# Four graph layers on one core: TensorE's loaded offsets without their comparisons against bounds

## The reference

```python
x = _layernorm(x + _L0_gnn_ref(x, src, dst, ...), axis=-1)      # degree-normed sum, then an MLP with gelu
x = _layernorm(x + _L1_gnn_ref(x, ..., src, dst, edge_type_8), axis=-1)   # relational attention, one head
x = _layernorm(x + _L2_gnn_ref(x, src, dst, ...), axis=-1)      # (1 + eps) * x + sum, then an MLP with relu
x = _layernorm(x + _L3_gnn_ref(x, edge_attr_64, src, dst, ...), axis=-1)  # attention, four heads, edge scores
```

## Time and profile before

| | us |
|---|---|
| median of 3 runs | 12608.17 (12603.52 to 12621.22) |
| the profiled execution, its own time | 12556.69 |
| its span on the core | 12555.0 |
| PE busy with matmuls | 4294.8 (34%) |
| ACT busy | 3446.0 (27%) |
| POOL busy | 6450.9 (51%) |
| DVE busy | 1628.9 (13%) |

### The profile page before, as it was taken

One profiled execution on the slowest core, in us unless ns is written; L12 is line 12 of the kernel. 1 busy time (PEld: TensorE's weight loads), 2 busy tenths in 40 slices (PEclk: granted clock), 3 DMA queues, 4 the chain that ended last, 5 costly groups with the idle time before them and its releaser, 6 DMA issues. The chain is left out here.

```text
span 12555.0 us, 93986 instructions
## 1 busy us (share of the span) xinstructions
PE 4294.8 (34%) x19065; PEld 3850.4 (31%) x19066; DVE 1628.9 (13%) x3883; ACT 3446.0 (27%) x9383; POOL 6450.9 (51%) x6784
## 2 busy tenths in 40 slices
PE   6233333352222232232244444444512222222222
PEld 5233332341222222222244444444412222222222
DVE  6000000013010110110100000000221111121113
ACT  1333333342222222222223223233312222222222
POOL 1666666656445445445355555555454444444442
PEclk6555555555555555555555555555555555555555
DMA  3111111112000000000111111111210111000110
GB/s 90 23 22 22 22 23 22 22 40 63 18 17 19 17 17 19 17 17 19 27 38 41 41 40 38 41 42 41 53 38 20 20 21 20 20 20 19 21 20 18
DMA packets 333875, 360.12 MB, mean 29 GB/s; under 512 B 172933, under 2 KB 205783, under 8 KB 330425
## 3 DMA queue, kind: packets, MB, share of 16 engines
q0 software_dynamic: 217552, 231.94, 9.4%
q1 hardware_dynamic: 116254, 127.34, 3.2%
HBM read 314.78 MB, written 46.51 MB: 29 GB/s over the span
## 5 line engine op out<-in xcount | busy, mean ns | idle before, releaser
L1037 POOL DMA_INDIRECT rows_a<-table,idx_c_a x3320 | 3166.1, 954 | 3380.4 <-ACT neg_c_a L999 2388.2
L839 POOL DMA_INDIRECT rows_l<-table,idx_c_l x3320 | 3140.1, 946 | 2349.8 <-ACT neg_c_l L793 1264.0
L587 PE MATMUL acc_l<-rows_l,hot_l 128*128 128x65 f32 x6640 | 1638.4, 419 | 2075.8 <-ACT hot_l L743 1226.6
L587 PEld LDWEIGHTS acc_l<-rows_l,hot_l 128*128 128x128 f32 x6640 | 1510.0, 328 | 2215.4 <-issue 2182.3
L587 PE MATMUL acc_a<-msg_a,hot_a 128*128 128x66 f32 (+1 forms) x6640 | 1612.1, 426 | 699.9 <-issue 520.7
L741 ACT ACTIVATE dist_a<-iota,neg_c_a 128x128 bf16<-128x128 f32 x3320 | 1050.9, 387 | 2664.3 <-remote 2286.5
L587 PEld LDWEIGHTS acc_a<-msg_a,hot_a 128*128 128x128 f32 x6640 | 1476.6, 328 | 833.0 <-issue 829.5
L1221 PE MATMUL work_a<-ident,tail_a 48*1 48x48 f32 (+3 forms) x140 | 32.7, 234 | 3410.9 <-DVE tail_a L1099 2844.2
L1221 PEld LDWEIGHTS work_a<-ident,tail_a 48*1 48x1 f32 (+3 forms) x140 | 10.8, 77 | 3439.6 <-issue 3439.6
L741 ACT ACTIVATE dist_l<-iota,neg_c_l 128x128 bf16<-128x128 f32 x3320 | 1049.9, 386 | 13.9 <-PE acc_l L587 8.5
L792 ACT COPY idx_c_l<-src_tl 128x16 int32 (+1 forms) x208 | 42.3, 204 | 3429.0 <-PE acc_l L587 1756.6
(11 more groups left out here) (258 smaller groups left out, 2499.2 us busy)
## 6 DMA issues: line engine op xcount, KB each, us to landing
rows_l<-table,idx_c_l POOLq DMA_INDIRECT x3320
rows_a<-table,idx_c_a POOLq DMA_INDIRECT x3320
feat<-edge_attr SPq DMA_DIRECT2D x25, 1125.0 KB
feat<-edge_attr SPq DMA_DIRECT2D x25, 937.5 KB
table<-stage SPq DMA_DIRECT2D x49, 260.0 KB
spread<-zero SPq DMA_DIRECT2D x12, 832.0 KB
starts_l<-spread SPq DMA_DIRECT2D x2, 3328.0 KB
we_v<-edge_s_l SPq DMA_DIRECT2D x1, 3328.0 KB
```

Of the source, the lines that this page charges most:

```text
L587: return nc.tensor.matmul(acc[:, bass.ds(at, row.shape[-1])], hot, row, start=False, stop=True, skip_group_check=True)
L839: pool.indirect_dma_start(rows[:, s, k, 0:D], None, table, bass.IndirectOffsetOnAxis(idx_c[:, s, k:k + 1], 0))\
L1037: pool.indirect_dma_start(rows[:, u, k, 0:row], None, table, bass.IndirectOffsetOnAxis(idx_c[:, u, k:k + 1], 0)).then_inc(gathered[u], 16)
```

## The change

The two calls by which PE loads offsets are given a reason for which the comparisons may be left out. Nothing else is altered: the loads, the order, all waits, and DVE's own load with its comparisons stay. The table `offs` is made as before; its block numbers were already held to 0..NB - 1.

```diff
         TOP = (NG - 1) * BANK + (BPB - 1) * AW
+        BOUNDED = "the table is worked out from a block number clamped to 0..NB - 1"
...
                                 _, at = nc.values_load_multi_w_load_instructions(
-                                    offs[0:1, bass.ds((i * SLOTS + s) * CH, CH)], engines=PE_ONLY, min_val=0, max_val=TOP)
+                                    offs[0:1, bass.ds((i * SLOTS + s) * CH, CH)], engines=PE_ONLY, min_val=0, max_val=TOP,
+                                    skip_runtime_bounds_check_because=BOUNDED)
...
                             return nc.values_load_multi_w_load_instructions(
-                                offs[0:1, bass.ds(g * S + lo, size)], engines=PE_ONLY, min_val=0, max_val=TOP)[1]
+                                offs[0:1, bass.ds(g * S + lo, size)], engines=PE_ONLY, min_val=0, max_val=TOP,
+                                    skip_runtime_bounds_check_because=BOUNDED)[1]
```

## The result

The changed kernel took **12280 us** (median of 4 runs, 12276.05 to 12293.82), the kernel before on the same chip 12610 (4 runs): ratio **0.974**, 95% interval 0.9723 to 0.9756. I had forecast 11995, with 11640 to 12340 as the range. The time lies where rival B put it, 12283. The change brought 330 us of the 613 I had summed up. The median of before has one run more than the 12608.17 above.

What follows compares the result with a forecast made beforehand. No engine is always busy; loops are bound by circles of waits, with slow spells during POOL's gather runs. Savings of 153, 56, 34, 83 and 287 summed to 613 us, taking the median 12608 to 11995, range 11640 to 12340.

Steps and rivals of the forecast that it cites:

- rival B: Gather loops of layers 0 and 2 barely move, attention gains 209: 325 us saved, 12283 us; chance 0.22.
- Step 1: Layer 1's second tail transpose no longer waits for comparisons: 4.5 us in each of 34 groups, -153 us.
- The rule that I had set against it: TENSOR_LOAD at about 200 ns a register: load 3.2 us, 2.7 us a group saved, sum 61 smaller.
- Step 2: Layer 3's second tail transpose: 1.66 us less waiting in each of 34 groups, -56 us.
- Step 3: First and third comparison sets of an attention group: first 0, third 1 us a group in layer 1, -34 us.
- Step 5: Layer 2's gather loop goes from 1.673 to 1.50 us a gather, -287 us, bounds -83 and -453.
- Step 4: Layer 0's gather loop gains 0.05 us a gather, -83 us, bounds -33 and -118.
- Slow spells: While POOL gathers without a pause, PE, ACT and their signals crawl, catching up afterwards: 1.40 us a gather against POOL's 1.25.
- C: Spells thin out with fewer PE instructions, loops reach POOL's 1.25 us a gather: 10990 us; chance 0.10.
- E: Slower: layer 0 and 2 visits come earlier and land in spells, 12690 us; sign: ACT's index copies wait longer; chance 0.05.

Runs made afterwards that it cites:

- second set alone: Kernel before with a quarter of the gathers, only the second of three comparison sets per attention group left out: 6337.3 us, 211 less than with all.
- quarter runs: Kernel before and changed kernel, each fetching one row of each four: 6548.6 and 6014.4 us; changed kernel with one-hots one chunk earlier as well: 5497.7 us.
- delayed pair: Kernel before and changed kernel, one row of each four fetched, ten chained ACT copies before the index copy in the gather loops: 7612.4 and 7255.2 us.

## Why the prediction was right and wrong

*The sum and the range.* The time fell into the range because the range had been drawn wide enough at its slow end for rival B, whose number it came to. The sum of 613 was 283 too large. The failed terms are steps 4 and 5: 370 us for the loops, where the layers show 26, 93 at most. That the error of the sum is no larger is chance: 31 us came outside the four stretches, where I had put nothing, and 67 in no layer that the traces show. (The range's quick end, 11640, was 22 us short of my own bound of 11618, which did no harm.)

*Step 1, layer 1's second tail transpose, -153: right.* The wait went from 4.92 to 0.42, and the layer gave 161 (4.7 a group). The rule that I had set against it, by which the load alone would have left 1.9 us of the wait, does not hold for this load: 16 registers out of SBUF in 1.10 us. The second set alone gave 148 where nothing else disturbed.

*Step 2, the same in layer 3, -56: right in what waits, a little large.* 45 in the kernel, 51 for that set alone. In both cases the argument was short and held: one engine compares, all others idle, and the row shows who waited.

*Step 3, the first and third sets, -34: too large by some 26, within its bounds.* Layer 1 gave 8 us more than step 1. The cover that I named, the late signal at the end of the run of gathers, did its work: the score still starts 8.9 us behind the last gather. That a cover and not cheapness hides them is seen where spells are missing and gathers few: there the change brought 191 us in layer 1 and 128 in layer 3, where the second set had 148 and 51. What the step said of the first set without its cover was wrong: it costs 0.9 us in layer 1 and nothing in layer 3, not the 4.5 and 1.7 of the second, because it runs mostly beside the last visits of the group before and beside DVE's work on the scores (in the run of the second set alone its load began at 2009.1 and its last assert at 2014.8, with visits until 2012.75 and DVE's first tails at 2014.0). The third costs 2.4 in either layer.

*Step 5, layer 2, -287: wrong, and the larger error.* The step said that "the comparisons stand exactly there, when PE is fast and POOL has just restarted", and drew from that that they lie in the circle. The place was right, the conclusion not. The earlier trace rows itself had the answer: the visits at 7408.15 were released by ACT's one-hots, [2.67 <-ACT hot_l L743], not by PE's own sequencer. The row of line 876 that I did not set beside it:

```profile
L876 PEldq SEQ_ASSERT  x16: 18/18/18, 7403.1 to 7407.4; - x16
L876 PEldq TENSOR_LOAD <-offs x1: 1107/1107/1107, 7401.7 to 7401.7; - x1
```

The load begins 3.9 us before ACT's copy at 7405.61, since PE's sequencer runs ahead of its array, which is busy with visits until 7405.47. The comparisons end at 7407.4, and ACT's one-hots come after that. The circle of the loops is PE's array, signal, ACT's copies and one-hots, PE's array; the register work lies on a chord of it, beside the way over ACT. By itself the chord is longer than ACT's way, by the 0.7 and 1.1 us a chunk that the quarter runs show, 70 and 110 us. With a signal that comes late it is shorter, and then it costs nothing. In layer 2 there is a second way beside it, over DVE's copies of the edge units. What PE waited for in that loop before (6396 to 8752 us):

```profile
PE turn L708 <- issue: 523.7, 58, 18.0
...
PE turn L708 <- DVE part L688: 387.4, 58, 13.9
...
PE acc_l L587 <- ACT hot_l L743: 240.8, 68, 11.6
```

and after (6190 to 8545):

```profile
PE turn L709 <- DVE part L689: 549.2, 58, 20.8
...
PE acc_l L588 <- ACT hot_l L744: 338.2, 77, 13.5
...
PE turn L709 <- issue: 195.7, 47, 20.8
```

The 328 us of "issue" that left the edge units' multiplies came back as waits for DVE (162 on this row, 70 on a smaller one) and for ACT (97): PE stood about as long as before.

*Step 4, layer 0, -83: wrong by the same conclusion.* Its bound of 0.02 a gather (33 us), for which it gave no working, was already over the 15 measured. In the kernel before, ACT's copy came over 5 us after PE's last visit in 72 of the 100 chunks of that loop that wait for one. After it did in 89 of 100:

```profile
1040.12 7.73 PE L588 MATMUL acc_l<-rows_l,hot_l 128*128 128x65 f32 x32 [14.85 <-ACT hot_l L744]
...
1057.24 0.20 ACT L793 COPY idx_c_l<-src_tl 128x16 int32 x1 [11.49 <-remote]
```

The visits end at 1047.85 and ACT copies at 1057.24. PE's wait for ACT's one-hots (line 588 in the page's row above, 1680.2 us) was 1226.6 on that row of the page of before: time of the comparisons became waiting. What PE's visits waited for in the loop of layer 0, before (511 to 2676 us) and after (500 to 2665):

```profile
PE acc_l L587 <- ACT hot_l L743: 801.8, 56, 17.3
PE acc_l L587 <- issue: 610.3, 246, 17.3
```

```profile
PE acc_l L588 <- ACT hot_l L744: 1123.9, 121, 26.0
PE acc_l L588 <- issue: 323.2, 43, 12.7
```

1412 us and 1447. In that loop line 876's comparisons and register arithmetic had taken 537 us in all, with the slow ones, and the loop came out 15 quicker (82 at most, were all of the 67 us above its own). So in the kernel itself, where it is slow, PE's register work was not what the loop waited for. That a late signal hides the comparisons in full is shown by the delayed pair, for a delay that I made; that it is the spells' late signals that do it in the original loops follows from their size, and was not tried by itself on such a chip. In layer 2 only 28 of 100 copies came that late (29 after), and most of the hiding is DVE's, whose copies wait for late signals in turn (line 693: "remote", 1388.9 us in 92 waits before; 1597.7 in 101 after).

*Slow spells.* I had taken it that PE, ACT and their signals crawl. Of PE, ACT and DVE only PE's sequencer did: the register instructions ahead of ACT's index copies took at most 0.06 us in the kernel before (line 792), and DVE's own asserts at most 0.041 (line 1143). And PE's crawl was not what the time hung on: it went with the comparisons, and what stayed, the late signals, still paces the loops at 1.46 and 1.65 us a gather and attention at 67.6 us from a run's first gather to the score.

*The rivals.* B had the right number, 325 against 330, by luck, and half the reason. Its attention of 209 came (206), but its loops of 116 were 26, and the rest is the 31 outside and the 67 that no layer shows. It named the spells' pace and the late copies, not ACT's one-hots. C came in its cause and not in its effect: a seventh fewer instructions took the crawl of PE's sequencer away and left the distance of 8.7 us, and so the time, as it was. Why the crawl went no run tells, and that it went is read from one profiled execution of either kernel. E did not come, though its sign to look for did: ACT's copies waited for late signals more often than before, at no cost, and no visits of layer 0 fell into a crawl, since there was none.

## What to carry to other kernels

Before an instruction is priced by where it stands, read what released the work behind it: a row that says ACT means that nothing of PE's sequencer was in the way. PE's sequencer ran ahead of its array here (by 3.8 us at 7401.7), so register work between two batches of matmuls starts before the first batch has ended, and is paid only where it outlasts the other engine's way back. A saving off the circle shows as another engine's wait growing by as much. That instructions are slow in a trace does not say that they are paid for either: 537 us of them went from layer 0's loop, and by the traces it gained 15.

Measure again where the bound is another one: this change was worth 2.6% where POOL had to wait for the others and 0.3% where it did not. And to see what a change does behind a cover, take the cover away, as with the quarter of the gathers.

## What the runs showed of the hardware

I had taken the slow spells for a property of the kernel. They belong to the place where it runs: the same program took 12610 and 12658 us in two sets of runs and 9007 to 9031 on three other chips, each set of runs steady to 0.4% (the profiled execution of before, 12557, lies 0.4% under its own), with nearly the same granted clock (0.505 to 0.506 and 0.507 to 0.510). Where it is slow, signals come late in the parts with twelve and more gathers in a row and not in those with four; the score starts 8.7 us behind a run of 48 gathers and 3.8 behind one of 12, which is 6.2 later than undisturbed. PE's sequencer crawled there too, at some 0.7 us an instruction, in the kernel with all comparisons (1,083 of 6,640 address instructions), and next to never in the changed one (11). POOL's own pace within a run is 1.25 us in both. What differs between these chips no run here tells, and nothing was tried on it.

ACT's order is a change for the next kernel: with one-hots one chunk earlier the loops fell from 10.4 to 7.9 us a chunk in layer 0 and from 14.4 to 11.8 in layer 2 with a quarter of the gathers (the gathers' spans from 1047.8 to 804.0 us and from 1430.1 to 1172.8). With all gathers and no spells it brought nothing that can be measured: 8992.7 with it, beside 8993.1 on the same chip for attention's comparisons out and 9006.5 in another place for the change alone. Whether it helps where spells are was not tried, so no version here is shown to beat the changed kernel.
